# Expert stage on sixteen unpadded sorted tiles: 23 jobs of tile and expert, rows kept on chip, and one routing program for two stages

## The reference

```
route = softmax(x @ router_w + router_b); max_prob = max(route); max_ind = argmax(route)
for e in range(8):
    a, g = split(x @ w1[e], 2)            # 128 -> 2 x 512
    y = silu(a) * g @ w2[e]               # 512 -> 128
    out = where(max_ind == e, y, out)
x = x + tanh(g_ffn[0]) * out * max_prob
```

## Time and profile before

| | before |
|---|---|
| median of 3 runs | 338.0 us (337.6 to 339.51) |
| the profiled execution | 338.46 us |
| its span, first to last instruction | 336.7 us |
| granted TensorE clock, mean of the span | 0.979 |
| busy: PE, DVE, ACT, POOL | 90%, 58%, 47%, 44% |
| first expert stage, first gather to last `y_gate` | 57.93 to 140.81 us |
| gathers and scatters in it | 23 and 23 |

### The profile page before, as it was taken

How to read it: one execution, slowest core, us unless ns; L and a number is a source line. 1 busy time by engine, 2 the same in 40 slices (tenths; PEclk the granted TensorE clock), 3 DMA queues, 4 the chain that set the end, 5 groups by cost and what they waited for, 6 DMA issues and landing times.

```text
span 336.7 us, 8511 instructions
## 1 busy us (share of the span) xinstructions
PE 302.7 (90%) x2895; PEld 246.3 (73%) x2907; DVE 196.5 (58%) x600; ACT 158.2 (47%) x336; POOL 148.4 (44%) x333
## 2 busy tenths in 40 slices
PE   8997997859999699998689998989779999999995
PEld 3646673659999699943366887867435999999995
DVE  7548958233433244346577887883686565555663
ACT  1263512101444355243286666769522655555661
POOL 7741501844666454322465556462114325543232
PEclk9999978987999999999999999999999999999999
DMA  7929985277322121143675665403994111111000
GB/s 200 359 72 352 369 248 154 64 156 154 82 64 65 54 57 38 33 131 99 160 165 145 163 155 135 111 7 101 281 301 137 35 45 50 50 47 41 19 17 25
DMA packets 35537, 41.60 MB, mean 124 GB/s; under 512 B 4780, under 2 KB 30415, under 8 KB 34335
## 3 DMA queue, kind: packets, MB, share of 16 engines
q1 hardware_dynamic: 29064, 31.81, 33.4%
q0 software_dynamic: 3120, 7.67, 8.2%
q10 hardware_dynamic: 3312, 1.58, 1.8%
HBM read 29.79 MB, written 10.96 MB: 121 GB/s over the span
## 4 chain that ended last, share of the span: by engine, by line
PE 67%; DVE 13%; POOL 5%; issue 4%; another core or an unknown queue 4%; DMA 3%; ACT 3%; SPq 0%; DVEq 0%; ACTq 0%; POOLq 0%
PE bank L1284 11%; PE pairA L1068 6%; PE pairA L1274 5%; PE bank L1077 5%; PE pairB L1274 5%; PE pairB L1068 5%; PE bank L1796 4%; PE pairA L1766 3%; PE pairB L1782 3%; DVE maxi L1866 2%; PE pairA L345 2%; PE pairB L345 2%; DMA x<-in_x 1%; POOL lnv L301 1%
## 5 line engine op out<-in xcount | busy, mean ns | idle before, releaser
L1866 DVE TENSOR_REDUCE maxi<-pairA 128x8 f32<-128x1024 f32 x30 | 36.7, 1222 | 14.2 <-PE pairA L1766 12.8
L1284 PE MATMUL bank<-wring,prob 128*128 (+1 forms) x312 | 42.0, 278 | 0.3
L1284 PEld LDWEIGHTS bank<-wring,prob 128*128 128x128 f32 x312 | 38.2, 192 | 1.8 <-issue 1.4
L1838 ACT ACTIVATE prob<-pairB 128x1024 f32<-128x1024 f32 x30 | 30.7, 1023 | 14.6 <-PE pairB L1782 14.6
L1178 POOL DMA_INDIRECT back_d<-ysb,inv_i x23 | 22.6, 983 | 28.9 <-DVE ysb L1139 25.8
L1173 POOL DMA_INDIRECT qs<-rows_b_d,inv_i x23 | 22.5, 978 | 22.7 <-DVE inv_i L767 16.2
L1425 POOL DMA_INDIRECT out_x<-qs,inv_i x16 | 15.7, 980 | 34.2 <-DVE qs L1379 34.2
L1145 DVE COPY xtT<-bank 128x128 f32<-128x128 f32 x23 | 6.7, 291 | 37.2 <-PE bank L1054 20.9
L301 POOL TENSOR_TENSOR lnv<-lnv,neg_half 128x4 f32<-128x4 f32 (+1 forms) x12 | 14.8, 1230 | 29.3 <-DVE lnv L296 29.3
L1334 ACT ACTIVATE xn<-wring 128x516 f32 x37 | 23.5, 634 | 7.6 <-issue 7.3
L1419 POOL DMA_INDIRECT qs<-rows_d_d,inv_i x16 | 15.5, 966 | 24.4 <-DVE big L1372 12.8
(11 more groups left out here) (338 smaller groups left out, 690.3 us busy)
## 6 DMA issues: line engine op xcount, KB each, us to landing
wring<-in_wts SPq DMA_DIRECT2D x8, 768.0 KB, 8.2
wring<-in_wts SPq DMA_DIRECT2D x8, 514.0 KB, 5.2
ks<-kparts_d SPq DMA_DIRECT2D x12, 192.0 KB
qs<-qparts_d SPq DMA_DIRECT2D x12, 192.0 KB
kparts_d<-parts SPq DMA_DIRECT2D x8, 192.0 KB, 2.5
qparts_d<-parts SPq DMA_DIRECT2D x8, 192.0 KB, 2.5
ctx_s<-kparts_d SPq DMA_DIRECT2D x6, 192.0 KB
ctxT<-qparts_d SPq DMA_DIRECT2D x6, 192.0 KB
```

Source lines behind the costliest of these rows:

```text
L1284: j = eng.matmul(bank[1 + i % 2][:, 0:D], act[:, i % 2, c_, :], down_weights(e, o), start=(c_ == 0), stop=(c_ == C1 - 1))
L1838: eng.activation(prob[:, at.half(5), :, :].rearrange("p h t -> p (h t)"), turned_in(at.unit(5))[:, :, :].rearrange("p a t -> p (a t)"), AC ...
L1866: eng.reduce_max(maxi[:, at.half(0), :], scores_in(at.unit(0))[:, :, :].rearrange("p a (h t) -> p (a h) t", t=T), AX).then_inc(s("mx"), 1)
```

## The change

`route_b` and `route_d` become one function `route(nth, jobs, fills, beside, behind)`. The first expert stage takes the form of the second: 16 sorted tiles in `xs`, and 16 + 8 - 1 = 23 jobs. `b_dve` now also makes `less_s`, the number of tokens with a smaller expert. All jobs but job 0 read their up weights through `copy_up`. The gates of the jobs come from the gates of the slots by a transpose and one product more (`gates_turned`, `job_gates`, `job_gate`). Gather t waits until tile t - 3 has been turned; three gathers go first, the gate work of POOL comes behind them. A tile is scattered once, four scatters between the last four gathers and twelve behind. The key loads still wait for `pmp`.

```diff
-    WARM = (26, 14, 16, 10, 30, 12, 3, 12, 4, 13, 6, 2, 18)
+    WARM = (26, 14, 16, 13, 30, 12, 3, 12, 4, 13, 6, 2, 18)
-    V_WARM, B_WARM = (20,), (4, 1, 2, 8)
+    V_WARM, B_WARM = (20,), (4, 1, 2, 5)
-        back_d = scratch("back_d", (NTOK + K * T, D))
+        back_d = scratch("back_d", (NTOK, D))
...
+            c.link(eng.scalar_tensor_tensor(less_h[:, :, :], bc(iota_p[:, 0:NE + 1], 1, NB), -float(NE), bc(r16[:, 2, :], 2, NE + 1), ALU.add, ALU.is_gt))
+            c.link(eng.tensor_reduce(less_f[:, :], less_h[:, :, :].rearrange("p b e -> p e b"), AX, ALU.add))
+            eng.tensor_copy(less_s[:, :], less_f[:, :]).then_inc(s("less"), 1)
...
+        gate_b, late_dve_b, late_pe_b = route(1, NIB + 1, (0, WARM[3], WARM[7], WARM[8]), gate_sums, gates_of)
...
+            def up(eng, i, tau):
+                wait(eng, n["xT"], min(i + 1, TT))
+                wait(eng, n["act"], i - 1)
+                if i == 0:
+                    wait(eng, w_in[0], 16)
+                    w = wring[:, 0, 0:2 * F0]
                 else:
+                    wait(eng, n["ups"], i)
+                    w = ups[:, i % 2, :]
...
             def pe(eng):
+                turn_over(eng, 0)
+                seg_pe(eng)
+                up(eng, 0, 0)
+                eng.wait_ge(s("te"), 1)
+                job_tiles = job_block(mybir.EngineType.PE, 0, 0, NIB)
+                turn_over(eng, 1)
+                gate_pe(eng)
+                for i in range(1, NIB):
+                    up(eng, i, job_tiles[i])
+                    if i == 1:
+                        expert = job_block(mybir.EngineType.PE, 1, 0, NIB)
+                        place_gates(eng)
...
+                    if i + 1 < TT:
+                        turn_over(eng, i + 1)
+                    if i == 2:
+                        gates_turned(eng)
+                    down(eng, i - 1, expert[i - 1])
+                    if i == 2:
+                        job_gates(eng)
+                down(eng, NIB - 1, expert[NIB - 1])
...
             def act_all(eng):
+                eng.wait_ge(s("rows_b"), 16 * 2 * G)
+                for e in range(NE):
+                    eng.wait_ge(w_in[e], 16)
+                eng.wait_ge(s("te"), 1)
+                expert = job_block(mybir.EngineType.Activation, 1, 0, NIB)
+                copy_up(eng, 1, expert[1])
+                copy_up(eng, 2, expert[2])
+                for i in range(NIB):
+                    wait(eng, n["h"], i + 1)
+                    wait(eng, n["act"], i - 1)
+                    eng.activation(sil[:, i % 2, :], (pairA, pairB)[i % 2][:, 0, :], ACT.Silu).then_inc(n["half"], 1)
...
             def pool(eng):
                 eng.wait_ge(s("gather"), 1)
                 eng.wait_ge(s("rows_b"), 16 * 2 * G)
-                for k in range(FIRST):
-                    gather(eng, Tile(k))
+                for t in range(FIRST):
+                    gather(eng, t)
                 gate_parts(eng)
-                for k in range(FIRST, AHEAD):
-                    gather(eng, Tile(k))
-                eng.wait_ge(s("scatter"), 1)
-                for k in range(K):
-                    if k + AHEAD < K:
-                        gather(eng, Tile(k + AHEAD))
-                    scatter(eng, Tile(k))
+                for t in range(FIRST, TT):
+                    eng.wait_ge(n["xT"], t - FIRST + 1)
+                    gather(eng, t)
+                    if t >= TT - LATE:
+                        scatter(eng, t - (TT - LATE))
+                for t in range(LATE, TT):
+                    scatter(eng, t)
```

More of the change, by code:

```diff
@@ L733, in xn_out, with route @@
             SP.append(sp)
-        def route_b(xn_ready):
-            rank_pe(1)
-            PE.append(lambda eng: warm(eng, bank[5], V_WARM[0]))
+        def route(nth, jobs, fills, beside, behind):
+            before_rank, ranked, placed, cast = fills
+            if before_rank:
+                PE.append(lambda eng: warm(eng, bank[7], before_rank))
+            rank_pe(nth)
+            earlier = nth - 1
+            end, grown, whole, over_by = (ends[:, k, :] for k in range(4))
+            base, crossed, first, back = of_tile[:, 0:2], of_tile[:, 2:4], of_tile[:, 4:5], of_tile[:, 5:6]
+            expert, wrap, away, low, gate = (job[:, k, 0:jobs] for k in range(5))
+            at_tile, at_back, segTp, of_job = bank[3][0:1, 0:jobs], bank[3][0:1, 64:64 + jobs], bank[3][0:TT, 128:128 + T], bank[3][:, 256:256 + jobs]
@@ L753, in dve @@
[L753 to L774, removed]
@@ L781, in dve @@
[L781 to L785, removed]
-            DV.append(dve)
-            def act(eng):
-                eng.wait_ge(s("tile"), 1)
-                eng.activation(ohk[:, :, 1, :], ohk[:, :, 0, :], ACT.Copy, scale=part[:, 0:1]).then_inc(s("hotk"), 1)
@@ L803, in route_b @@
-            PE.append(pe2)
-            xn_out("b", xn_ready)
-        def route_d():
-            PE.append(lambda eng: warm(eng, bank[7], WARM[12]))
-            rank_pe(2)
-            KT = TT
-            end, grown, whole, over_by = (ends[:, k, :] for k in range(4))
-            base, crossed, first, back = of_tile[:, 0:2], of_tile[:, 2:4], of_tile[:, 4:5], of_tile[:, 5:6]
-            expert, wrap, away, low, gate = (job[:, k, :] for k in range(5))
-            at_tile, at_back, segTp, of_job = bank[3][0:1, 0:NJ], bank[3][0:1, 64:64 + NJ], bank[3][0:TT, 128:128 + T], bank[3][:, 256:256 + NJ]
-            def dve(eng):
-                c = chain(eng, "dve")
-                eng.wait_ge(s("rank"), 2)
+                eng.wait_ge(s("rank"), nth)
@@ L887, in pe2 @@
                                    start=(b == 0), stop=(b == NB - 1))
                 i.then_inc(s("inv"), 1)
-                warm(eng, bank[5], WARM[7])
-                eng.wait_ge(s("job_made"), 1)
-                eng.matmul(at_tile, part[0:TT, :], begun[:, 2, :], start=True, stop=True)
-                eng.matmul(at_back, back, begun[:, 2, :], start=True, stop=True).then_inc(s("job_sums"), 1)
-                warm(eng, bank[5], WARM[8])
+                warm(eng, bank[5], placed)
+                eng.wait_ge(s("job_made"), 3 * earlier + 1)
@@ L894, in route_d @@
+                eng.matmul(at_tile, part[0:TT, :], begun[:, 2, 0:jobs], start=True, stop=True)
+                eng.matmul(at_back, back, begun[:, 2, 0:jobs], start=True, stop=True).then_inc(s("job_sums"), 1)
+                warm(eng, bank[5], cast)
             PE.append(pe2)
             def seg_pe(eng):
-                eng.wait_ge(s("job_made"), 2)
+                eng.wait_ge(s("job_made"), 3 * earlier + 2)
                 eng.transpose(segTp, seg[:, :], ident[:, :]).then_inc(s("job_sums"), 1)
@@ L900, in gate_pe @@
             def gate_pe(eng):
-                eng.wait_ge(s("job_made"), 3)
-                eng.matmul(of_job, segT[:, :], begun[:, 2, :], start=True, stop=True).then_inc(s("job_sums"), 1)
-            return gate, (seg_dve, gate_dve), (seg_pe, gate_pe)
+                eng.wait_ge(s("job_made"), 3 * earlier + 3)
+                eng.matmul(of_job, segT[:, :], begun[:, 2, 0:jobs], start=True, stop=True).then_inc(s("job_sums"), 1)
+            return gate, (seg_dve, (mask_dve, half_dve)[earlier]), (seg_pe, gate_pe)
@@ L1133, in experts_b @@
[L1133 to L1145 removed]
+                j.then_inc(s("pmp"), 1)
@@ L1169, in experts_b, with job_gate, add_job @@
-            DV.append(tiles(dve_step))
+                eng.tensor_tensor(pm[:, 0, :], pm[:, 0, :], pm[:, 2, :], ALU.add).then_inc(s("gate_made"), 1)
+            def job_gate(eng):
+                c = chain(eng, "dve")
+                eng.wait_ge(s("gate_sums"), 2)
+                eng.wait_ge(s("gate_made"), 1)
+                c.link(eng.tensor_tensor(gate, gate_p, mask, ALU.mult))
+            def add_job(eng, i, tau):
+                kept = tile_of(xs, tau, D)
+                wait(eng, n["yp"], i + 1)
+                wait(eng, n["y"], i)
+                eng.scalar_tensor_tensor(kept, bank[1 + i % 2][:, 0:D], gate[:, i:i + 1], kept, ALU.mult, ALU.add).then_inc(n["y"], 1)
```

364 lines of the change are left out of this document (150 added, 214 removed).

## The result

The changed kernel takes 327.81 us (median of 4, 327.18 to 329.51); the kernel before, run beside it, takes 338.75 (median of 4, 337.6 to 341.92). The ratio is 0.967, with an interval of 0.9592 to 0.9749. The forecast was 327.0 with a range of 322.5 to 335.5. The profiled execution took 328.26 with a span of 326.5.

What follows compares the result with a forecast made beforehand. TensorE, busy 90% of the span, was taken as the bound, with 12.1 us lost around first-stage pauses. Terms 1.9 - 0.6 + 0.8 + 12.1 = 14.2, less 1.2 and 1.5, gave 11.5 gained: 327 us, range 322.5 to 335.5.

Steps and rivals of the forecast that it cites:

- Indices 2.7 us earlier: Routing before the first expert stage: shorter routing plus gate sums takes 4.86 + 0.15 us instead of 7.70.
- the start of the stretch: TensorE's products ahead of the ranks: two short ones more, three fill products fewer; called even, 0.4 either side.
- up(0) 2.2 earlier: First up product of the first expert stage: at 59.5 instead of 61.70, after `gates_of` 0.25 and 4.29 from the indices.
- The first three jobs: Start of the first expert stage: weight copies, then the Silu table load, give back 0.3; gate work in job 2 loses 0.6.
- The jobs: First expert stage: still 23 jobs, transposes fall from 23 to 16, gain 0.8 us.
- 1.2 + 1.5 = 2.7 charged: Deductions in the first expert stage: 1.2 us for small delays between jobs, 1.5 for late gathers.
- rival C: First expert stage: paced gathers come late under key loads and TensorE's clock drops; 6.3 gained, time 332; chance 0.2.
- The 12.1 us: Time lost around first-stage pauses without releaser; expected to go by likeness to the second stage, bounds 0 to 12.1.
- 11.5 was forecast: Total gain at the end of the first expert stage: 14.2 - 1.2 - 1.5 = 11.5 us.
- The tail from up(22): End of the first expert stage, last up product to last result: kept unchanged at 4.84 us.
- my first theory: Theory 1 of the experiments, first expert stage: pauses come from how far gathers run ahead; most of 12 us.
- rival B: First expert stage: pauses return because TensorE's job stream is nearly the same; gain 2.1, time 336; chance 0.2.

Runs made afterwards that it cites:

- first runs: The kernel before, unedited, as profiled ahead of the change: profiled execution 338.46 us, median 338.0.
- all three, B: The changed kernel with the Silu table loaded early, key loads late and gathers five ahead instead of three, on the second chip: 324.76 us, ratio 0.9624.
- before again, A: The kernel before with no edit, run again for its trace on the first chip: 327.69 us (one run), span 326.0.
- before, keys late, A: The kernel before with the attention key loads held back until 17 tiles of the first expert stage are turned: 326.25 us, ratio 0.9969.
- on A: Chip of the first group of follow-up kernels; the unedited kernel before took 328.36 us there (13 runs, 325.26 to 340.02).
- on C: Chip of the third group of follow-up kernels; the unedited kernel before took 339.07 us there (12 runs, 336.3 to 353.98).
- on B: Chip of the second group of follow-up kernels; the unedited kernel before took 338.07 us there (11 runs, 334.39 to 343.32).

## Why the prediction was right, point by point

**Indices 2.7 us earlier.** The stretch was put at 4.86 + 0.15 and took 4.90. Relative to the logits the indices came 12.53 - 9.14 = 3.4 earlier. The rest is the start of the stretch, which I called even: it came 0.6 earlier (4.24 us behind the logits, 4.83 before).

**up(0) 2.2 earlier.** It was 3.35, relative to the logits. Besides the 0.6, from the indices to up(0) it took 4.12 us, not 0.25 + 4.29: `gates_of` found room beside the job list. The step was right in kind, 1.1 too small.

**The first three jobs.** up(0) to up(2) took 7.02 us, where I had 6.7, and 6.38 before. Copies, table load and Silu stood in the order that was written, and up(2) to up(3) took 3.32, where 2.79 + 0.6 was expected.

**The jobs.** 2.79 and 2.68, with 16 transposes, as forecast. From up(3) to up(22) it took 126.06 - 70.01 = 56.05 us; even jobs make 12 x 2.79 + 7 x 2.68 = 52.24. The 3.8 between stand against 1.2 + 1.5 = 2.7 charged. They are 2.1 about the late gather (4.58 + 2.99 for two jobs of 2.79, and 0.1 more) and 1.7 in jobs 11 and 13. The gather landed after 9.55 us, beyond the 8.1 that I took from the row writes as the worst. TensorE waited for a gather only once, but others may have been as slow: with six ahead seven of them took 8.1 to 11.0 us. The key loads are what makes them late. This was rival C at a third of its price, and TensorE's clock did not fall for it: the window from 76 to 78, at 0.50 before, has 1.00.

**The 12.1 us.** This is nearly the whole gain, and it went. With all terms the stage ends 10.95 us earlier, where 11.5 was forecast; the gain of up(0), 1.1 too small, and the charges, 1.1 too small, cancel by luck. The tail from up(22) to the last result took 5.12 us, where 4.84 was kept. The ground for the 12.1 was likeness to the second stage, not a mechanism. The runs show what the likeness was worth. I set beside each other every row of five or more indirect transfers that POOL issues back to back, 1.25 to 1.40 us from start to start, in the first stage:

| kernel, chip | row of transfers | piece without releaser, us |
|---|---|---|
| before, first runs | 5 from 66.61 | 5.25 |
| before, first runs | 6 from 103.53 | 4.37 |
| all three, B | 5 from 61.83 | 2.54 |
| six ahead, table early, scatters behind, C | 6 from 61.70 | 5.75 |
| changed, scatters behind, C | 6 from 96.36 | 2.98 + 2.19 |
| before, scatters behind, C | 19 from 113.50 | 16.17 (and 1.6 lost in the job before) |
| before again, A | 6 from 69.56 | none |
| before, five ahead, A | 6 from 72.38 | none |
| before, keys late, A | 6 from 69.47 | none |
| changed, six ahead, A | 7 from 61.54 | none |

A piece is not the loss itself: ordinary work lies in it, and slow work follows. In the kernel before, 3.7 and 2.7 us are lost in the two jobs from up(2) to up(4) by the first pause and the slow clock behind it, and 3.4 from up(13) to up(14) by the one at 107.87. Its row and what waits behind it:

```profile
103.53 0.98 POOL L1178 DMA_INDIRECT back_d<-ysb,inv_i  x1 [1.62 <-DVE ysb L1139]
...
109.96 0.97 POOL L1173 DMA_INDIRECT qs<-rows_b_d,inv_i  x1 [0.30 <-issue]
112.23 0.60 ACT L1117 ACTIVATE prob<-pairB 128x512 f32<-128x512 f32 x1 [5.06 <-remote]
```

The third piece of the earlier trace rows, 2.25 us from 100.63, is not in the table: it stands beside a row of four (from 97.09), and up(11) to up(12) takes 3.19 us, so only 0.4 is lost. The kernel before has three more rows of four at this spacing, beside which a job loses between 0.1 and 0.5. The bound of 1.40 us matters too: on A the kernel before issues up to 36 transfers at no more than 1.50 us (from 65.49, keys late), and its jobs stay at 2.79.

The changed kernel has no row of more than three in this stage, and no pause in either of its profiled runs. Three edits put a long row at a place where there had been none (scatters behind, in both kernels, and six ahead), and each made a pause at that place on C, as five ahead did on B. One of the three took the rows's stretches away, and those pauses went. It is not that a pause lets work pile up for POOL: in the row of 19 it is the order of the program that holds the scatters back, until their results lie ready. So on chips of this kind long rows bring the pauses, and it follows, though no run has the kernel before with nothing but the pacing, that the pacing is what removed them, by keeping POOL's indirect transfers apart. The number of transfers ahead, my first theory, is not it: six and five ahead without a pause on A. Nor is it the program's TensorE stream, on which rival B rested: the pause follows POOL's instructions from place to place, and the same stream runs without it on A. Nor the fetch of its instructions, which B drew from the Trainium skill (Runtime: NRT & Kernel Launch, Instruction fetch mechanics): the instruction queues have their blocks, but none moves at the end of the 16 us, nor anywhere near the pause at 107.87. In the changed kernel with all scatters behind a block does move inside the pause, at 100.96, so these two pauses are the ones that speak against the fetch.

**What stays open.** The rows and pauses go together and the edits move both, but nothing in the trace says what of POOL's work holds TensorE, from how long a row on, nor why chip A is spared. A run of the changed kernel without an edit on A was not made, so its gain there is known only with six ahead: 1.3%, not 3.3. The prediction's range did hold, but it knew nothing of such chips: the gain that it forecast is conditional on the pauses of the earlier trace rows, and in its words "the step on the 12.1" is the one that falls where they don't occur.

## What to carry to other kernels

When the chain has pieces without a releaser, look at what the other queues issue in just that stretch, and run the kernel again on another chip before a gain is promised from them. Pace indirect transfers to the consumer, with a lead that covers the slowest landing (four tiles here, 11.2 us at 2.79 a job, for a landing of 9.6), and let neither gathers nor scatters pile up into a burst. Starting the other large loads behind the last gathers took the waits away as well, since it is they that make gathers late.

## What the hardware showed that I had not expected

The same kernel took 328.4 us on one chip and 338 to 339 on others, with granted clocks near 0.98 on either; the trace shows the difference as pauses of TensorE. Such a pause can last 16 us while the DMA engines are at a share of 0.15. In five of the six rows with a pause the piece ends 1.2 to 2.4 us after POOL is done with the row; in the row of five on B it ends before, at 66.00. One gather of 128 rows, 3.05 us when alone, took 9.3 to 13.0 us beside the key loads.
